# Query and key weight columns permuted at the split, so that a row's rotary partner lies in the next PSUM bank

## The chip, the cores and the metric

The kernel runs on one core of one Trainium2 chip. The metric is the device time of one execution in microseconds (us), the median of several runs.

## The reference, cut to what matters

Two layers over 4 batches of 512 tokens with 512 features, in float32. The first attends from the tokens to 1601 context rows and gates the result. The second has a causal self-attention with 16 heads of 32 features, a cross-attention and a feed-forward part. The change lies in the second layer's queries and keys:

```python
x = rms_norm(hidden_states, ln_in_w)
mixed = jnp.where(vm, x @ v_qkv, x @ l_qkv)      # two experts, chosen by token
q, k, v = jnp.split(mixed, 3, axis=-1)
...
def rotate_half(x):                               # x: ... x 32 (one head)
    d = x.shape[-1] // 2
    return jnp.concatenate([-x[..., d:], x[..., :d]], axis=-1)
...
return (q * cos + rotate_half(q) * sin, k * cos + rotate_half(k) * sin)
```

Feature f of a head (f below 16) is thus paired with feature f + 16 of the same head, and `cos` and `sin` repeat with a period of 16 features.

## The kernel before

All matrix products are made from float32 values that are split into a high and a low part (`hi`, `lo`, type fp32r), with three matmuls for each product (`three`, lines 106 to 108). The program is a sequence of stages, each a block with one instruction list for each engine; semaphores alone order the engines, and each engine takes its list in order. Between stages stands a barrier.

The stage of the change is `queries_values_keys`. It goes over the four batches in four turns (`i` = 0 to 3, batch `turns[i]`). A turn has three parts on TensorE: queries (part 0), values (part 1) and keys (part 2); the last turn takes keys before values (`place`). A part adds up eight steps (two experts of four weight tiles each) into four of the eight PSUM banks, and the parts alternate between the two halves (`bank`). In a query or key part, bank `j` ends up with features 128 j to 128 j + 127 as rows and 512 tokens as columns. For the second expert only 128 of the 512 tokens are computed here, since the branch for late tokens is taken.

The rotation of a query or key part goes as follows. ScalarE copies the four banks to `plain` (`keep_plain`, L840). TensorE multiplies each of them with the constant 128 x 128 matrix `rot`, which swaps the halves of each head and negates one, in float32, back into the same bank (`rotate`, L1097, two matmul records for each call); these calls stand between the first two steps of the next part. GpSimd forms `t1 = plain * cos_r` (`scale_pieces`, L931), with three buffers: the fourth piece has to wait until the first piece's store from `t1` has landed. VectorE multiplies the bank with `sin_r` into `plain` (L1017), adds it to `t1` (L1020), and forms the low part (L1024) after ScalarE has rounded the high part (`round_piece`, L847). SyncE stores both parts to DRAM (`store_piece`, L754 and L756), 128 rows of 2 KB at a time.

The row statistics of the norm are made meanwhile. ScalarE squares, GpSimd adds (L920), TensorE sums over the rows (`sums`, L1105) after the fourth step of the query part, ScalarE takes logarithm and exponential (`root`, L860 and L862), VectorE makes the second statistics (`second_sums`, L995 and L998) and the scaled tables (`tables`, to L1007). A little matmul (L1130) turns the row scales into a column, which VectorE copies (L1050, `rs_col`).

What lets a part begin: the query part needs the split input of its step and the value banks copied out; the value part (in the last turn the key part) needs the second statistics and all key banks of the turn before used by VectorE (`s_t2`); the key part needs all query banks used and `rs_col` copied. On ScalarE, `round_piece` of the third and fourth key piece stands behind the first `root` of the next turn.

The weights of the stage are loaded to `w_raw` (four buffers) and split: the first four tiles by VectorE at the end of the stage before (`split_tile`, L367 and L369), the other 20 by ScalarE (`round_w`, L812) and VectorE (`rest_w`, L968) in the first turn.

Of the kernel before, what the change touches and what calls it, by code (L numbers as in the profile page):

```python
# [7 lines left out]
P = 128  # L8
# [16 lines left out]
def program(nc, t, out):  # L25
# [21 lines left out]
    with ExitStack() as keep:  # L47
# [10 lines left out]
        mask_qk, mask_kq = sb("mask_qk", [P, 4, P], bf16), sb("mask_kq", [P, 4, P], bf16)  # L58
        rot = sb("rot", [P, P])
        cos_t, sin_t = sb("cos_t", [P, S]), sb("sin_t", [P, S])  # L60
# [43 lines left out]
        def three(dst, ah, al, bh, bl, start, stop, **how):  # L104

            nc.tensor.matmul(dst, ah, bh, start=start, stop=False, **how)  # L106
            nc.tensor.matmul(dst, al, bh, start=False, stop=False, **how)  # L107
            return nc.tensor.matmul(dst, ah, bl, start=False, stop=stop, **how)  # L108

        WSEMS = " ".join(f"s_wl{i}" for i in range(RAW)) + " s_wh s_ws s_wu "  # L110


        def gated_context():
# [23 lines left out]
            with ctx:  # L137
# [33 lines left out]
                with nc.Block() as block:  # L171
                    @block.sync
                    def _(sp):
# [38 lines left out]
                        for b in range(B):  # L212
                            if b:
                                sp.wait_ge(s["s_g"], 2 * DT * b)
                                sp.dma_start(fused_d[b - 1], h[:, :, :]).then_inc(s["s_up"], 16)
                            if b and b + 1 < B:
                                load_x(b + 1)
                            if b == B - 1:
                                sp.wait_ge(s["s_tl"], NB * B)
                                sp.dma_start(posi, t["pos_1xS"].broadcast_to((P, S))).then_inc(s["s_pos"], 16)  # L220
                                sp.dma_start(tpos[:, :], t["c_tpos"]).then_inc(s["s_pos"], 16)
                                sp.dma_start(tab, t["c_tab"].rearrange("(a p) c n -> p a c n", p=P)).then_inc(s["s_pos"], 16)
                                sp.dma_start(masks, t["c_masks"]).then_inc(s["s_pos"], 16)
                                sp.dma_start(tti, t["mask_BxS_ik0"][B - 1].rearrange("(a n) -> a n", a=1).broadcast_to((P, S)))\
                                    .then_inc(s["s_tt"], 16)
                                sp.dma_start(rot[:, :], t["c_rot"]).then_inc(s["s_pos"], 16)
                                sp.dma_start(sel[:, :], t["c_sel"]).then_inc(s["s_pos"], 16)
                            for p in range(2, len(PIECES)):
                                load_rows(len(PIECES) * b + p)
                            if b + 1 < B:  # L230
                                load_context(b + 1)
                                for p in range(2):
                                    load_rows(len(PIECES) * (b + 1) + p)
                        sp.wait_ge(s["s_csl"], len(PIECES) * B)
                        for n in range(DT + ET, len(tiles)):
                            load_w(sp, n, tiles[n], wl, s["s_ws"])
                        sp.wait_ge(s["s_pos"], 96)
                        sp.wait_ge(s["s_up"], 16 * (B - 1))
# [96 lines left out]
                    def _(dve):  # L335
# [21 lines left out]
                        def split_tile(n):  # L357
# [5 lines left out]
                            else:  # L363
                                hi, lo = w_hi[:, n - DT - ET, :], w_lo[:, n - DT - ET, :]
                                dve.wait_ge(s["s_gx"], DT * B)
                            dve.wait_ge(wl[n % RAW], 16 * (n // RAW + 1))
                            nc.vector.tensor_copy(hi, w_raw[:, n % RAW, :]).then_inc(s["s_wh"], 1)  # L367
                            dve.wait_ge(s["s_wh"], n + 1)
                            nc.vector.tensor_tensor(out=lo, in0=w_raw[:, n % RAW, :], in1=hi.bitcast(f32), op=ALU.subtract)\  # L369
                                .then_inc(s["s_ws"], 1)  # L370
# [21 lines left out]
                        def positions():  # L392

                            dve.wait_ge(s["s_pos"], 96)
                            nc.vector.tensor_copy(posf, posi).then_inc(s["s_hot"], 1)
# [293 lines left out]
        def queries_values_keys(more_h, more_l, k_r, q_r, v_r, s_key, s_value, s_first):  # L689

            names = ("s_tt s_k s_ku0 s_ku1 s_eu s_hin s_x s_xh s_xl s_sq s_sum s_ss s_rs s_tab s_r0u s_pl s_rot s_t1 s_t2 s_rp s_rh s_rl "
                     "s_uh0 s_uh1 s_ul0 s_ul1 s_ul2 s_rc s_rcc s_vn s_uv0 s_uv1 s_hup " + WSEMS)
# [12 lines left out]
            with ctx:  # L705
# [18 lines left out]
                def done(i, part):  # L724

                    return NT * i + G * (place(i, part) + 1)

                def split_of(n):

                    return (w_hi[:, n, :], w_lo[:, n, :]) if n < SPLIT else (more_h[:, n - SPLIT, :], more_l[:, n - SPLIT, :])  # L730

                with nc.Block() as block:
                    @block.sync
                    def _(sp):
# [14 lines left out]
                        def store_piece(o):  # L749
# [3 lines left out]
                            sp.wait_ge(s["s_rh"], o + 1)  # L753
                            sp.dma_start(dst[turns[i], 0, k * P:(k + 1) * P, :], hi[:, o % 2, :].bitcast(f32)).then_inc(s_uh[o % 2], 16)  # L754
                            sp.wait_ge(s["s_rl"], o + 1)
                            sp.dma_start(dst[turns[i], 1, k * P:(k + 1) * P, :], t1[:, o % 3, :]).then_inc(s_ul[o % 3], 16)  # L756

# [50 lines left out]
                    def _(act):  # L808
                        def round_w(n):

                            act.wait_ge(wl[n % RAW], 16 * (n // RAW))
                            nc.scalar.activation(split_of(n)[0], w_raw[:, n % RAW, :], ACT.Copy).then_inc(s["s_wh"], 1)  # L812

# [130 lines left out]
                    def _(dve):  # L944
# [64 lines left out]
                        def turn_pieces(i, group):  # L1009

                            dve.wait_ge(s["s_tab"], 5 * (i + 1))
                            for j in range(DT + 1):
                                o = 2 * DT * i + DT * group + j
                                if j < DT:
                                    dve.wait_ge(s["s_rot"], o + 1)
                                    dve.wait_ge(s["s_t1"], o + 1)
                                    nc.vector.tensor_tensor(out=plain[:, j, :], in0=ps[:, bank(3 * i + place(i, 2 * group), j), :], in1=sin_r[:, :],  # L1017
                                                            op=ALU.mult).then_inc(s["s_t2"], 1)
                                    dve.wait_ge(s["s_t2"], o + 1)
                                    nc.vector.tensor_tensor(out=t1[:, o % 3, :], in0=t1[:, o % 3, :], in1=plain[:, j, :], op=ALU.add)\  # L1020
                                        .then_inc(s["s_rp"], 1)
                                if j:
# [37 lines left out]
                    def _(pe):  # L1060
# [31 lines left out]

                        def rotate(i, group, j):

                            o = 2 * DT * i + DT * group + j
                            pe.wait_ge(s["s_pl"], o + 1)
                            nc.tensor.matmul(ps[:, bank(3 * i + place(i, 2 * group), j), :], rot[:, :], plain[:, j, :], start=True, stop=True)\  # L1097
                                .then_inc(s["s_rot"], 1)

                        def sums(i, n):  # L1100

                            pe.wait_ge(s["s_sum"], 3 * (2 * i + n + 1))
                            if i:
                                pe.wait_ge(s["s_t2"], 2 * DT * (i - 1) + DT + n + 1)
                            nc.tensor.matmul(ps[:, bank(3 * i + 1, n), :], ones[:, :], sq[:, 2 + n, :], start=True, stop=True)\  # L1105
                                .then_inc(s["s_ss"], 1)

                        def run(i, t0, steps):

                            parts = (0, 2, 1) if i == B - 1 else (0, 1, 2)  # L1110
                            for m in steps:
                                step, n = m % G, G * parts[m // G] + m % G
# [1456 lines left out]
def constants():  # L2569
# [4 lines left out]

    rot = np.zeros((P, P), np.float32)
    low = p % HD < HD // 2
    rot[p[low] + HD // 2, p[low]] = -1.0
    rot[p[~low] - HD // 2, p[~low]] = 1.0
    c["c_rot"] = rot

    c["c_sel"] = (p[:, None] == np.array([[HD * h for h in range(4)] + [HD * h + CHD for h in range(4)]])).astype(np.float32)
# [41 lines left out]
```

## Time and profile before

| | |
|---|---|
| Median of 3 runs | 2180.31 us (2179.99 to 2183.4) |
| Span of the profiled execution | 2183.6 us; no other time of that execution is listed |
| TensorE, busy share of the span | 93% |
| VectorE, ScalarE, GpSimd, busy share | 68%, 46%, 23% |
| Mean granted TensorE clock | 0.954 |
| The stage of the change | from some 358 to 620 us |

The span runs from the first to the last instruction of one profiled execution. Busy times of TensorE are modelled ends of pipelined matmuls, so distances between starts are the surer measure. A granted clock of 1.00 is the level of 2.4 GHz, one of 0.50 that of 1.2 GHz.

### The profile page before, as it was taken

To read this page: it belongs to the slowest core of one execution; us is meant where nothing else is said; L and a number is where in the kernel's file an instruction comes from. 1 tells how busy PE (TensorE), PEld (TensorE's weight loads), DVE (VectorE), ACT (ScalarE), POOL (GpSimd) and SP (SyncE) were. 2 spreads that over 40 slices of the span, in tenths; PEclk is the share of its full clock that TensorE was granted. 3 is DMA by queue.
4 is the path that set the end of the run, shared out by engine and by line. 5 is a ranking of instruction groups with operands and counts; after the bars stand their busy time and mean duration, and the time that the engine had idled before them with its cause. 6 is when DMAs were issued, how large, how long until landed. Compare 5 with 4: busy or idle time off the path is not lost. (4 is left out here: it accounts for less than half of the span.)

```text
span 2183.6 us, 32815 instructions
## 1 busy us (share of the span) xinstructions
PE 2022.3 (93%) x12701; PEld 1349.4 (62%) x12718; DVE 1492.5 (68%) x2047; ACT 1006.7 (46%) x1748; POOL 503.2 (23%) x496
## 2 busy tenths in 40 slices
PE   6999997899979997888889999999998899999997
PEld 5788874677755554677634444444434678778885
DVE  5776786566547775656579999999952565866563
ACT  1333314445415554444348888888884222221111
POOL 0321231133301212332201213222132212221211
PEclk9999998799979999999979999999999899999999
DMA  3222112333367662585544354453501433344332
GB/s 139 70 99 80 40 53 86 113 122 122 99 173 171 171 166 87 207 263 195 156 124 84 71 97 83 78 98 69 97 17 26 124 88 102 98 110 112 99 94 58
DMA packets 174936, 236.99 MB, mean 109 GB/s; under 512 B 26234, under 2 KB 103166, under 8 KB 172570
## 3 DMA queue, kind: packets, MB, share of 16 engines
q1 hardware_dynamic: 166624, 223.71, 38.2%
q0 software_dynamic: 7856, 10.90, 1.8%
q8 instruction: 113, 1.85, 0.4%
q14 instruction: 55, 0.45, 0.1%
q10 hardware_dynamic: 288, 0.08, 0.0%
HBM read 169.61 MB, written 62.91 MB: 106 GB/s over the span
## 5 line engine op out<-in xcount | busy, mean ns | idle before, releaser
L2133 ACT ACTIVATE pT_x<-ps 128x512 f32<-128x512 f32 (+1 forms) x832 | 451.3, 595 | 85.3 <-PE ps L2231 57.6
L2172 DVE TENSOR_REDUCE quarters<-ps 128x2 f32<-128x804 f32 x480 | 454.4, 992 | 46.1 <-PE ps L2203 45.0
L2246 PE MATMUL ps<-pT_x,vx_ring 128*17 128x256 f32 (+1 forms) x3328 | 261.9, 388 | 0.2 <-ACT osb_x L2115 0.2
L106 PE MATMUL ps<-mi_h,w_hi 128*128 128x512 f32 (+1 forms) x440 | 174.0, 396 | 10.5 <-DVE mi_l L2427 10.5
L2392 POOL TENSOR_TENSOR sg<-sg,keep_all 128x512 f32<-128x512 f32 (+1 forms) x55 | 87.8, 1595 | 386.5 <-ACT sg L2371 386.5
L107 PE MATMUL ps<-mi_h,w_lo 128*128 128x512 f32 (+1 forms) x440 | 173.4, 394 | 0.0
L108 PE MATMUL ps<-mi_l,w_hi 128*128 128x512 f32 (+1 forms) x440 | 172.8, 393 | 0.0
L1320 DVE TENSOR_REDUCE row_max_s<-ps 128x1 f32<-128x384 f32 (+3 forms) x176 | 109.5, 633 | 67.9 <-PE ps L1352 67.1
L1292 ACT ACTIVATE pT_s<-ps 128x512 f32<-128x512 f32 (+1 forms) x176 | 96.0, 558 | 114.9 <-PE ps L1377 112.8
L100 DVE CAST w_hi<-w_raw 128x512 fp32r<-128x512 f32 (+1 forms) x165 | 84.4, 511 | 71.5 <-PE ps L108 65.5
L2246 PEld LDWEIGHTS ps<-pT_x,vx_ring 128*17 128x17 f32 (+1 forms) x3328 | 55.6, 95 | 110.9 <-issue 68.5
L102 DVE TENSOR_TENSOR w_lo<-w_raw,w_hi 128x512 fp32r<-128x512 f32 (+1 forms) x165 | 115.8, 702 | 5.7
L2375 ACT ACTIVATE hid_h<-prod 128x512 fp32r<-128x512 f32 (+1 forms) x55 | 34.9, 634 | 177.5 <-DVE prod L2455 177.5
L2371 ACT ACTIVATE sg<-ps 128x512 f32<-128x512 f32 (+1 forms) x55 | 32.8, 596 | 164.4 <-PE ps L108 164.4
L291 ACT ACTIVATE pT<-ps 128x512 f32<-128x512 f32 (+1 forms) x52 | 31.0, 598 | 158.0 <-PE ps L108 158.0
L106 PEld LDWEIGHTS ps<-mi_h,w_hi 128*128 128x128 f32 (+1 forms) x440 | 82.3, 187 | 31.0 <-issue 11.5
L1352 PE MATMUL ps<-qkv_h,qkv_l 96*128 96x128 f32 (+3 forms) x256 | 90.5, 414 | 10.1 <-PEq L76 7.8
L108 PEld LDWEIGHTS ps<-mi_l,w_hi 128*128 128x128 f32 (+1 forms) x440 | 82.3, 187 | 20.1
L107 PEld LDWEIGHTS ps<-mi_h,w_lo 128*128 128x128 f32 (+1 forms) x440 | 82.3, 187 | 18.8
L2455 DVE TENSOR_TENSOR prod<-ps,sg 128x512 f32<-128x512 f32 (+1 forms) x55 | 37.9, 690 | 78.8 <-PE ps L108 70.0
L106 PE MATMUL ps<-hid_h,w_hi 128*128 128x512 f32 (+1 forms) x220 | 87.9, 400 | 3.0 <-DVE hid_l L2459 3.0
L331 POOL TENSOR_TENSOR sin_t<-sin_t,pT 128x512 f32<-128x512 f32 (+1 forms) x48 | 72.4, 1509 | 65.0 <-ACT pT L291 64.4
(350 smaller groups left out, 4816.6 us busy)
## 6 DMA issues: line engine op xcount, KB each, us to landing
qkv_l<-self_q_by_part SPq DMA_DIRECT2D x48, 256.0 KB, 4.5
qkv_h<-self_k_by_part SPq DMA_DIRECT2D x48, 256.0 KB, 6.6
w_raw<-L_xattn_l_gate SPq DMA_DIRECT2D x40, 256.0 KB, 2.9
w_raw<-L_xattn_l_up SPq DMA_DIRECT2D x40, 256.0 KB, 2.9
w_raw<-L_xattn_l_down SPq DMA_DIRECT2D x40, 256.0 KB, 2.7
kx_first<-cross_k_by_part SPq DMA_DIRECT2D x36, 200.2 KB, 6.7
cross_v_by_group<-v_aug SPq DMA_DIRECT2D x16, 442.0 KB, 3.8
vx_ring<-cross_v_by_group SPq DMA_DIRECT2D x16, 442.0 KB, 10.0
```

What stands on the lines that cost most here:

```text
L100: nc.vector.tensor_copy(hi, raw).then_inc(s_high, 1)
L102: nc.vector.tensor_tensor(out=lo, in0=raw, in1=hi.bitcast(f32), op=ALU.subtract).then_inc(s_split, 1)
L106: nc.tensor.matmul(dst, ah, bh, start=start, stop=False, **how)
L107: nc.tensor.matmul(dst, al, bh, start=False, stop=False, **how)
L108: return nc.tensor.matmul(dst, ah, bl, start=False, stop=stop, **how)
L1292: nc.scalar.activation(pT[:, u % 3, j:j + n, 0:width], heads_of(ps[:, SCORES + v % 3, :], n, width), ACT.Exp, scale=SCALE).then_inc(s["s_e ...
L1320: nc.vector.tensor_reduce(out=row_max[:, g % 2, j:j + heads, q], in_=heads_of(bank, heads, (q + 1) * P), axis=AX.X, op=ALU.max)\
L1352: last = nc.tensor.matmul(bank[:, m * width:(m + 1) * width], q_r[0:STACK, at + m, cut], k_r[0:STACK, at + m, 0:width], start=False, stop= ...
L2133: nc.scalar.activation(pT[0:kn, u % 3, j, :], ps[0:kn, 5 + v % 3, :], ACT.Exp, scale=SCALE)\
L2172: nc.vector.tensor_reduce(out=quarters[:, g % 2, pair, :, q, quarter], in_=ps[:, at:at + 2, 0:MAXW], axis=AX.X, op=ALU.max)\
L2246: last = nc.tensor.matmul(ps[j * HD:j * HD + CHD + 1, 4, queries], v_r[0:kn, g % RING, kt, j, :], pT[0:kn, u % 3, j, queries], start=kt == ...
L2392: nc.gpsimd.tensor_tensor(out=by_batch(sg[0:cn, c % 2, :]), in0=by_batch(sg[0:cn, c % 2, :]), in1=keep_all[0:cn, experts[i], :, rows(i)], ...
```

## The change

The columns of the query and key weights are written in another order when they are split: column 64 a + 16 q + r goes to column 128 q + 16 a + r (`p (a q r) -> p q a r`, with a below 8, q below 4, r below 16). Bank q then holds the features 64 a + 16 q + r, in row 16 a + r. The partner of a row lies in the same row of bank `q ^ 1`, and the tables need no change, as they depend on r alone. VectorE reads the partner's bank directly (L1017) and adds or subtracts (L1020). The rotation matmuls, the matrix `rot` and its load are gone. The stores put the rows back in their old places in DRAM, so that everything behind the stage is as it was. Two waits of TensorE now ask for the second used bank, and VectorE waits for the copy of the neighbouring bank ahead of an even piece.

```diff
+        def by_piece(w):
+            return w.rearrange("p (a q r) -> p q a r", q=DT, r=HD // 2)
...
-                                sp.dma_start(rot[:, :], t["c_rot"]).then_inc(s["s_pos"], 16)
...
+                            raw = w_raw[:, n % RAW, :]
+                            if n >= DT + ET:
+                                raw, hi, lo = by_piece(raw), *(w.rearrange("p (q a r) -> p q a r", q=DT, r=HD // 2) for w in (hi, lo))
-                            nc.vector.tensor_copy(hi, w_raw[:, n % RAW, :]).then_inc(s["s_wh"], 1)
+                            nc.vector.tensor_copy(hi, raw).then_inc(s["s_wh"], 1)
...
+                def piece_rows(dst, i, part, j):
+                    return dst[turns[i], part].rearrange("(a q r) n -> q a r n", q=DT, r=HD // 2)[j]
+                def raw_of(n):
+                    raw = w_raw[:, n % RAW, :]
+                    return raw if n // G == 1 else by_piece(raw)
+                def as_raw(w, n):
+                    return w if n // G == 1 else w.rearrange("p (q a r) -> p q a r", q=DT, r=HD // 2)
...
-                            sp.dma_start(dst[turns[i], 0, k * P:(k + 1) * P, :], hi[:, o % 2, :].bitcast(f32)).then_inc(s_uh[o % 2], 16)
+                            sp.dma_start(piece_rows(dst, i, 0, k), hi[:, o % 2, :].bitcast(f32)).then_inc(s_uh[o % 2], 16)
-                            sp.dma_start(dst[turns[i], 1, k * P:(k + 1) * P, :], t1[:, o % 3, :]).then_inc(s_ul[o % 3], 16)
+                            sp.dma_start(piece_rows(dst, i, 1, k), t1[:, o % 3, :]).then_inc(s_ul[o % 3], 16)
...
-                            nc.scalar.activation(split_of(n)[0], w_raw[:, n % RAW, :], ACT.Copy).then_inc(s["s_wh"], 1)
+                            nc.scalar.activation(as_raw(split_of(n)[0], n), raw_of(n), ACT.Copy).then_inc(s["s_wh"], 1)
...
-                            nc.vector.tensor_tensor(out=lo_, in0=w_raw[:, n % RAW, :], in1=hi_.bitcast(f32), op=ALU.subtract)\
+                            nc.vector.tensor_tensor(out=as_raw(lo_, n), in0=raw_of(n), in1=as_raw(hi_.bitcast(f32), n), op=ALU.subtract)\
...
-                                    dve.wait_ge(s["s_rot"], o + 1)
                                     dve.wait_ge(s["s_t1"], o + 1)
-                                    nc.vector.tensor_tensor(out=plain[:, j, :], in0=ps[:, bank(3 * i + place(i, 2 * group), j), :], in1=sin_r[:, :],
-                                                            op=ALU.mult).then_inc(s["s_t2"], 1)
+                                    if j % 2 == 0:
+                                        dve.wait_ge(s["s_pl"], o + 2)
+                                    nc.vector.tensor_tensor(out=plain[:, j, :], in0=ps[:, bank(3 * i + place(i, 2 * group), j ^ 1), :],
+                                                            in1=sin_r[:, :], op=ALU.mult).then_inc(s["s_t2"], 1)
...
+                                                            op=ALU.add if j % 2 else ALU.subtract).then_inc(s["s_rp"], 1)
...
-                                pe.wait_ge(s["s_t2"], 2 * DT * (i - 1) + DT + n + 1)
+                                pe.wait_ge(s["s_t2"], 2 * DT * (i - 1) + DT + 2)
...
-                                if m < 2 and i:
-                                    rotate(i - 1, 1, 2 * m)
-                                    rotate(i - 1, 1, 2 * m + 1)
...
-                                if m // G == 1 and step < 2:
-                                    rotate(i, 0, 2 * step)
-                                    rotate(i, 0, 2 * step + 1)
-                                if i == B - 1 and m // G == 2 and step < 2:
-                                    rotate(i, 1, 2 * step)
-                                    rotate(i, 1, 2 * step + 1)
...
-                                    pe.wait_ge(s["s_t2"], 2 * DT * i + DT * (place(i, 1) - 1) + 1)
+                                    pe.wait_ge(s["s_t2"], 2 * DT * i + DT * (place(i, 1) - 1) + 2)
```

## Rows read from the trace of the kernel before

**Rows 1.** The page, the span in 40 slices, TensorE's busy tenths.
```profile
PE   6999997899979997888889999999998899999997
```

**Rows 2.** Windows: stretch, length, busy time of each engine, clock, DMA share, GB/s.
```profile
530.00:560.00 30.00, 29.45 (x154) 24.14 (x153) 21.73 (x29) 15.21 (x26) 10.85 (x8) 1.00 0.28 97
```

**Rows 3.** Grouped lines of 330 to 625 us: busy us, mean ns, idle before.
```profile
L1097 PE MATMUL ps<-plain,rot 128*128 128x512 f32 x64 | 30.7, 602 | 2.2 <-ACT plain L840 2.2
...
L968 DVE TENSOR_TENSOR qkv_l<-w_raw,qkv_h 128x512 fp32r<-128x512 f32 x20 | 19.7, 1016 | 16.6 <-ACT qkv_h L812 16.6
```

**Rows 4.** Timeline of TensorE around two pairs of rotations: start, length, instruction.
```profile
442.75 1.98 PE L1097 MATMUL ps<-plain,rot 128*128 128x512 f32 x4 [0.55 <-ACT plain L840]
...
447.12 0.40 PE L108 MATMUL ps<-xe0l,w_hi 128*128 128x512 f32 x1
447.36 1.88 PE L1097 MATMUL ps<-plain,rot 128*128 128x512 f32 x4
...
449.30 0.40 PE L107 MATMUL ps<-xe0h,w_lo 128*128 128x512 f32 x1
```

**Rows 5.** Timeline of TensorE, third and fourth turn: first matmuls of parts, sums.
```profile
496.74 0.45 PE L106 MATMUL ps<-xe0h,w_hi 128*128 128x512 f32 x1
...
512.23 1.88 PE L1105 MATMUL ps<-sq,ones 128*128 128x512 f32 x4
...
519.26 0.46 PE L106 MATMUL ps<-qkv_h,xe0h 128*128 128x512 f32 x1
...
538.09 0.39 PE L106 MATMUL ps<-xe0h,qkv_h 128*128 128x512 f32 x1
...
554.28 0.45 PE L106 MATMUL ps<-xe0h,w_hi 128*128 128x512 f32 x1
...
576.80 0.46 PE L106 MATMUL ps<-xe0h,qkv_h 128*128 128x512 f32 x1
...
597.03 0.45 PE L106 MATMUL ps<-qkv_h,xe0h 128*128 128x512 f32 x1
```

**Rows 6.** Timelines of ScalarE, GpSimd and VectorE, third turn, query part.
```profile
513.29 0.69 ACT L860 ACTIVATE rs<-ps,eps_col 128x512 f32<-128x512 f32 x1 [4.73 <-PE ps L1105]
...
515.83 1.14 ACT L847 ACTIVATE rows_h<-t 128x512 fp32r<-128x512 f32 x2
...
509.45 1.29 POOL L931 TENSOR_TENSOR t<-plain,cos_r 128x512 f32<-128x512 f32 x1 [3.40 <-DMA self_k_by_part<-t]
...
511.57 0.69 DVE L1020 TENSOR_TENSOR t<-t,plain 128x512 f32<-128x512 f32 x1
516.47 1.29 DVE L1024 TENSOR_TENSOR t<-t,rows_h 128x512 fp32r<-128x512 f32 x2 [4.21 <-ACT rows_h L847]
...
518.47 0.69 DVE L998 TENSOR_TENSOR rs<-rs,ps 128x512 f32<-128x512 f32 x1
```

**Rows 7.** Timeline of VectorE, third turn, end of the value part.
```profile
534.33 1.47 DVE L1024 TENSOR_TENSOR t<-t,rows_h 128x512 fp32r<-128x512 f32 x2
536.03 0.16 DVE L1050 COPY rs_col<-ps 128x4 f32<-128x4 f32 x1 [0.24 <-PE ps L1130]
```

**Rows 8.** DMA issues (size, median us to landing), and a window within one store.
```profile
qkv_l<-self_q_by_part SPq DMA_DIRECT2D x48, 256.0 KB, 4.5
...
self_k_by_part<-t SPq DMA_DIRECT2D x16, 256.0 KB, 2.1
...
564.20:564.40 0.20, 0.20 (x2) 0.17 (x1) 0.20 (x1) 0.20 (x1) 0.00 (x0) 1.00 0.99 379
```

**Rows 9.** Two gaps of TensorE in the timeline, and windows behind them.
```profile
342.00 0.51 PE L106 MATMUL ps<-cn_h,w_h 128*128 128x512 f32 x1 [2.17 <-DVE cn_l L510]
...
345.00:352.00 7.00, 7.00 (x32) 5.63 (x31) 2.56 (x4) 2.75 (x4) 0.00 (x0) 1.00 0.00 0
...
421.30 0.47 PE L106 MATMUL ps<-xe0h,qkv_h 128*128 128x512 f32 x1 [1.83 <-DVE rs_col L1050]
...
422.50:426.00 3.50, 3.50 (x10) 2.71 (x9) 2.20 (x5) 0.01 (x1) 0.00 (x0) 0.52 0.75 230
```

More of the change, by code:

```diff
@@ L58, in program @@
         mask_qk, mask_kq = sb("mask_qk", [P, 4, P], bf16), sb("mask_kq", [P, 4, P], bf16)
-        rot = sb("rot", [P, P])
         cos_t, sin_t = sb("cos_t", [P, S]), sb("sin_t", [P, S])
@@ L236, in _ @@
                             load_w(sp, n, tiles[n], wl, s["s_ws"])
-                        sp.wait_ge(s["s_pos"], 96)
+                        sp.wait_ge(s["s_pos"], 80)
                         sp.wait_ge(s["s_up"], 16 * (B - 1))
@@ L366, in split_tile @@
                             dve.wait_ge(wl[n % RAW], 16 * (n // RAW + 1))
-                            nc.vector.tensor_copy(hi, w_raw[:, n % RAW, :]).then_inc(s["s_wh"], 1)
+                            raw = w_raw[:, n % RAW, :]
+                            if n >= DT + ET:
+                                raw, hi, lo = by_piece(raw), *(w.rearrange("p (q a r) -> p q a r", q=DT, r=HD // 2) for w in (hi, lo))
+                            nc.vector.tensor_copy(hi, raw).then_inc(s["s_wh"], 1)
                             dve.wait_ge(s["s_wh"], n + 1)
-                            nc.vector.tensor_tensor(out=lo, in0=w_raw[:, n % RAW, :], in1=hi.bitcast(f32), op=ALU.subtract)\
+                            nc.vector.tensor_tensor(out=lo, in0=raw, in1=hi.bitcast(f32), op=ALU.subtract)\
                                 .then_inc(s["s_ws"], 1)
@@ L392, in positions @@
                         def positions():
-                            dve.wait_ge(s["s_pos"], 96)
+                            dve.wait_ge(s["s_pos"], 80)
                             nc.vector.tensor_copy(posf, posi).then_inc(s["s_hot"], 1)
@@ L689, in queries_values_keys @@
         def queries_values_keys(more_h, more_l, k_r, q_r, v_r, s_key, s_value, s_first):
-            names = ("s_tt s_k s_ku0 s_ku1 s_eu s_hin s_x s_xh s_xl s_sq s_sum s_ss s_rs s_tab s_r0u s_pl s_rot s_t1 s_t2 s_rp s_rh s_rl "
+            names = ("s_tt s_k s_ku0 s_ku1 s_eu s_hin s_x s_xh s_xl s_sq s_sum s_ss s_rs s_tab s_r0u s_pl s_t1 s_t2 s_rp s_rh s_rl "
                      "s_uh0 s_uh1 s_ul0 s_ul1 s_ul2 s_rc s_rcc s_vn s_uv0 s_uv1 s_hup " + WSEMS)
@@ L1014, in turn_pieces @@
                                 if j < DT:
-                                    dve.wait_ge(s["s_rot"], o + 1)
                                     dve.wait_ge(s["s_t1"], o + 1)
-                                    nc.vector.tensor_tensor(out=plain[:, j, :], in0=ps[:, bank(3 * i + place(i, 2 * group), j), :], in1=sin_r[:, :],
-                                                            op=ALU.mult).then_inc(s["s_t2"], 1)
+                                    if j % 2 == 0:
+                                        dve.wait_ge(s["s_pl"], o + 2)
+                                    nc.vector.tensor_tensor(out=plain[:, j, :], in0=ps[:, bank(3 * i + place(i, 2 * group), j ^ 1), :],
+                                                            in1=sin_r[:, :], op=ALU.mult).then_inc(s["s_t2"], 1)
                                     dve.wait_ge(s["s_t2"], o + 1)
-                                    nc.vector.tensor_tensor(out=t1[:, o % 3, :], in0=t1[:, o % 3, :], in1=plain[:, j, :], op=ALU.add)\
-                                        .then_inc(s["s_rp"], 1)
+                                    nc.vector.tensor_tensor(out=t1[:, o % 3, :], in0=t1[:, o % 3, :], in1=plain[:, j, :],
+                                                            op=ALU.add if j % 2 else ALU.subtract).then_inc(s["s_rp"], 1)
                                 if j:
@@ L1091, in project @@
                             last.then_inc(s["s_wu"], 1)
[L1093 to L1098, printed above, removed]
                         def sums(i, n):
@@ L1111, in run @@
                             for m in steps:
-                                step, n = m % G, G * parts[m // G] + m % G
+                                n = G * parts[m // G] + m % G
                                 project(i, n, t0)
-                                if m < 2 and i:
-                                    rotate(i - 1, 1, 2 * m)
-                                    rotate(i - 1, 1, 2 * m + 1)
                                 if m == 3:
@@ L2573, in constants @@
     c = {"c_ident": np.eye(P, dtype=np.float32)}
[L2575 to L2579, printed above, removed]
     c["c_sel"] = (p[:, None] == np.array([[HD * h for h in range(4)] + [HD * h + CHD for h in range(4)]])).astype(np.float32)
```

## The prediction

> **What bounds the kernel now.** I read the page's slices first [rows 1]: TensorE is at 9 tenths in most of the 40 slices, the other engines nowhere for long, so the question is whether it is also the bound in the one stage that the diff touches. That stage (queries, values, keys of the self-attention) runs from about 358 to 620 us, in four turns of three parts each. In a stretch of its steady turns TensorE works 29.45 of 30.00 us at full clock, VectorE 21.73, ScalarE 15.21, GpSimd 10.85 [rows 2]. The grouped lines then give the size of what goes: 64 matmul records (two for each of 32 rotations), 30.7 us busy, and 2.2 us of waiting ahead of them [rows 3]. The timeline of TensorE shows that they stand in its stream like any other matmul, and where each part begins [rows 4, 5]; the timelines of the other engines show when the next part could begin [rows 6, 7]. The reader is to see that the parts start when TensorE is ready, but that the hand-back of PSUM banks follows closely.
>
> **What the removed work costs.** A pair of rotations lies between a matmul that starts at 447.12 and one at 449.30, with one projection matmul behind the pair: 2.18 us, less two normal steps of 0.23 each, is 1.71 us [rows 4]. There are 16 pairs: 27.4 us. With the waits of 2.2 us ahead of seven of them [rows 3], 29.6 us is the most that can come back. It comes back only where the next part can start earlier, so I walk through a steady turn, the third (its query part starts at 496.74 [rows 5]).
>
> **Query part to value part.** The value part waits for the row statistics (the second L998 result), which VectorE ends at 518.47 + 0.69 = 519.16; it starts at 519.26 [rows 5, 6]. VectorE reaches that result late because of a queue on ScalarE: the rounding of pieces 3 and 4 stands behind the logarithm, which waited 4.73 us for the sums of TensorE, and these stand behind both pairs of rotations [rows 5, 6]. Without them the sums move from 512.23 to 508.26 (2 x 1.71 and the wait of 0.55 [rows 4]); logarithm, rounding and statistics follow, 3.97 us earlier, to 515.2. What is late next is the last piece itself: its addition ends at 511.57 + 0.69 = 512.26 whatever TensorE does, because GpSimd waited 3.40 us for the store that frees its buffer [rows 6]; rounding (0.6) and the 2.19 us from its end (515.83 + 1.14) to the statistics give 515.1. TensorE itself would be ready at 519.26 - 3.97 = 515.29. So all 3.97 us come back, with about 0.1 us to spare.
>
> **Value part to key part.** The key part needs VectorE to have used all query banks and to have copied the row scales. VectorE ends its pieces at 534.33 + 1.47 = 535.80 [rows 7], 16.64 us behind the statistics, in a chain through ScalarE, GpSimd and a store in which no rotation is waited for; with the copy (0.16) and a semaphore it is 16.9. The key part could then start at 515.2 + 16.9 = 532.1 instead of 538.09: 6.0 us for the turn. TensorE is ready at 515.29 + 18.83 - 3.6 = 530.5, so 1.6 us of the second two pairs turn into a wait for VectorE. The key part holds no rotation and keeps its 16.19 us (538.09 to 554.28 [rows 5]).
>
> **The moved store.** A piece's 128 rows now go to eight blocks of 16 rows in DRAM, where they went to one block. A store of the old form fills its engines (share 0.99) and moves 256 KB in some 0.68 us at 379 GB/s, landing 2.1 us after its issue [rows 8]. No row shows the new form. Below it costs nothing (same bytes, same 2 KB rows); above, the nearest row is the load that gathers the same 256 KB in pieces from the same tensor: 4.5 us [rows 8], 2.4 more. I take 0.7 us, a doubled transfer, nearer to the store's own row because the loads come in bursts of six that queue behind each other. This lies on the path twice in a turn: the fourth product of GpSimd waits for the first store. The statistics come 0.6 us later (the spare 0.1 taken off), the row scales 0.7 more: 6.0 becomes 4.7 us in turns two and three. The row shows 16 engines at work. The Trainium skill, DMA: Bandwidth & Descriptors, section "Why a DMA increments its semaphore by 16 and not by 1", says that a transfer is spread over the largest count up to 16 that divides the outermost size of both sides; eight blocks would then use 8 engines. By that rule the sum is the one below; by the old store's row unchanged, it is 3.9 us better (0.7 + 1.3 + 1.3 + 0.6 over the turns); no run here shows it yet.
>
> **First and last turn.** The first key part already waits 1.83 us for the row scales [rows 9]. Its chain is set by VectorE's weight splits and a store, so the two pairs removed ahead of it only widen the gap to 5.3 us: gain 0, less 0.7 for the store. The last turn has keys before values: its query part gives 3.4; its key part (two pairs and a short wait, 3.6) has the banks in time, as VectorE has used them before 534.33, 15.2 us behind the statistics [rows 6, 7], and the part runs 597.03 - 576.80 - 3.6 = 16.6 [rows 5]; its value part gives 3.4. Together 10.4 us. What follows the stage (stores, barrier, loads) shifts as it is.
>
> **The clock.** After the gap of 1.83 us the granted clock was 0.52 (the 1.2 GHz level) for 3.5 us; after one of 2.17 us it stayed at 1.00 [rows 9]. At 0.52 the stretch loses 0.48 x 3.5 = 1.7 us. The new gaps are some 2.2 us in turns two and three and 5.3 us in the first. I charge 1.7 for one of the two, as one of the two rows fell, and 1.7 for the longer one: 3.4 us. Below 0, above 5.1.
>
> **The rest, at nothing.** The splits of the 16 permuted tiles handle as many elements as before, in runs of 16. No row shows that form; below it is free, above I double the mean of 1016 ns [rows 3]: eight tiles lie ahead of the first turn's pieces, at most 8.1 us. I take 0, since the element count sets the even duration of these rows. The added VectorE wait (the neighbour's eviction before an even piece) is covered by GpSimd's product of 1.29 us [rows 6], longer than one ScalarE pass (0.69 at most [rows 6]); uncovered, the subtraction, the remainder and the store behind it would wait too. The sums now wait for two used banks; the second is used long before 508. The dropped load of the rotation matrix (64 KB, one SP issue) lies among loads with slack.
>
> **The sum.** -0.7 + 4.7 + 4.7 + 10.4 - 3.4 = 15.7 us. The profiled execution spans 2183.6 us, 3.3 above the median of the runs (2180.31) and level with the slowest, 2183.4; its span becomes 2167.9, and the median 2164.6.
>
> **The rivals.**
> - *The store lands as before and the gaps leave the clock alone*: 0 + 6.0 + 6.0 + 11.0 = 23.0, 2157.3 us. For it: bytes and row length are unchanged, and one gap of 2.17 did no harm. Against: the other did. Chance 0.2.
> - *The store lands as late as the piecewise loads* (+2.4 us): the turns give -2.4, 1.3, 1.3, 8.7, less 3.4 for the clock: 5.5, 2174.8. Much the same would come of doubled splits (15.7 - 8.1 = 7.6, 2172.7). Together 0.18.
> - *The rotations were not on the path*: if the parts were paced by VectorE, SP's queue or the stores throughout, removal makes idle time only, and the time is 2180. Against: TensorE shows no idle ahead of the value part or the key part of the steady turns [rows 5]. Chance 0.04.
> - *Slower: the clock does not come back.* The rotations closed gaps; without them each key part of the first three turns begins after a wait. If its clock then stays at the 1.2 GHz level through the whole part, 16.19 us of work take about 15 us more, 45 in all: 2180.3 - 19.1 + 45 = 2206. It decides from 19.1 / 3 = 6.4 us lost in each, that is some 13 us at that level, four times the stretch of [rows 9]. Chance 0.06.
>
> My forecast has 0.5, and its own range is 2160 to 2169; 0.02 is left for what I don't see. The range that leaves out no more than 2 in 10 reaches from the best case to the doubled splits: 2156 to 2173. A measurement of this kernel tells about 0.2% (4.4 us) from no change. Faster by more: the first two cases and nearly all of the third, 0.89; within: 0.04; slower: 0.07.
>
> **What would show it.** Right: no rotation records; each steady turn (key start to key start) some 53 us instead of 57.5; the sums directly behind the fourth step; a wait of 1.5 to 2.5 us for the row-scale copy ahead of the key part in turns two and three, over 4 us in the first; none in the last turn. The store step is judged by the landing of the first store of a part (2.1 or 2.8 us) and by the DMA share while it runs (1.0 or 0.5); the split step by the mean of L968's successor. Wrong: low clock through key parts, a wait ahead of value parts over 1 us, splits above 1.3 us each, or an unchanged turn.

## The result and the profile after the change

The changed kernel takes 2202.39 us (median of 4 runs, 2199.21 to 2204.67) against 2180.88 for the one before (4 runs): a ratio of 1.0094, 95% interval 1.0079 to 1.0108. It is 1% slower; 2164.6 us had been forecast, with 2156 to 2173 as the range. The profiled execution took 2204.67 us (span 2202.7).

The rotations are gone, and nothing stands in their place on TensorE. Yet the third turn, query start to query start, is 62.24 us long where [rows 5] give 57.54. The timeline of the changed kernel for that turn, TensorE first, then ScalarE, GpSimd, VectorE and SyncE's issues (start, length, instruction, idle time before it and what ended that):

```profile
500.12 0.45 PE L105 MATMUL ps<-xe0h,w_hi 128*128 128x512 f32 x1
513.46 2.73 PE L1117 MATMUL ps<-sq,ones 128*128 128x512 f32 x4 [1.91 <-DVE plain L1036]
518.01 0.47 PE L105 MATMUL ps<-xe1h,qkv_h 128*128 128x128 f32 x1 [1.82 <-issue]
528.30 0.73 PE L105 MATMUL ps<-qkv_h,xe0h 128*128 128x512 f32 x1
546.07 0.47 PE L105 MATMUL ps<-xe0h,qkv_h 128*128 128x512 f32 x1 [1.20 <-DVE rs_col L1069]
562.36 0.46 PE L105 MATMUL ps<-xe0h,w_hi 128*128 128x512 f32 x1
...
640.87 1.31 PE L1355 MATMUL ps<-qkv_h,qkv_l 96*128 96x128 f32 x4 [18.25 <-PEq L75]
...
492.02 1.41 ACT L890 ACTIVATE v_nat<-ps,rs_col 128x512 f32<-128x512 f32 x2 [6.98 <-DMA self_v_by_group<-v_nat]
...
509.65 4.19 POOL L949 TENSOR_TENSOR t<-plain,cos_r 128x512 f32<-128x512 f32 x3
520.59 1.27 POOL L949 TENSOR_TENSOR t<-plain,cos_r 128x512 f32<-128x512 f32 x1 [6.75 <-DMA self_k_by_part<-t]
...
525.40 0.69 DVE L1016 TENSOR_TENSOR rs<-rs,ps 128x512 f32<-128x512 f32 x1
...
513.40 0.59 SPq L772 DMA_DIRECT2D self_k_by_part<-rows_h  x1
```

From the timelines of before, the lines to hold against it (ScalarE just ahead of the third turn, GpSimd in it, TensorE at the end of the stage):

```profile
483.97 1.42 ACT L872 ACTIVATE v_nat<-ps,rs_col 128x512 f32<-128x512 f32 x2 [1.96 <-DMA self_v_by_group<-v_nat]
...
501.81 4.24 POOL L931 TENSOR_TENSOR t<-plain,cos_r 128x512 f32<-128x512 f32 x3
...
623.39 1.31 PE L1352 MATMUL ps<-qkv_h,qkv_l 96*128 96x128 f32 x4 [7.76 <-PEq L76]
```

Read the first timeline from the bottom up. A store costs SyncE 0.59 us to issue. GpSimd's fourth product waits 6.75 us for the first store, where it waited 3.40 [rows 6]; the statistics end at 526.09, 25.97 us into the turn (22.42 before [rows 5, 6]). The value stores stand behind these stores on SyncE's list, so ScalarE waits 6.98 us for a value buffer (1.96 before). Behind that wait stand the next turn's rounding and squares: GpSimd's first product starts 9.53 us into the turn (5.07 before). So VectorE frees the banks late, and the statistics' matmuls wait 1.91 us for them. Behind them a second gap opens, 1.82 us that the view calls issue. The windows of the same kernel show what follows these gaps (stretch, length, busy time of each engine, granted clock, DMA share, GB/s):

```profile
515.20:515.40 0.20, 0.20 (x2) 0.00 (x0) 0.20 (x1) 0.20 (x1) 0.00 (x0) 0.50 0.60 102
518.01:528.30 10.29, 10.29 (x48) 10.29 (x49) 3.96 (x6) 5.55 (x8) 1.27 (x1) 0.50 0.49 142
```

The second expert of the query part runs its whole 10.29 us at a granted clock of 0.50, the 1.2 GHz level; that part took 5.71 us before (519.26 less the 513.55 at which it began, 1.32 us behind the sums of [rows 5]). While stores run, the DMA share is 0.5 to 0.6, at 102 GB/s in a stretch within a store, where [rows 8] show 0.99 and 379. At the end of the stage TensorE waits 18.25 us for the next stage's first matmul, where it waited 7.76.

### The profile page after: what moved, and what is told of

Read it like the earlier page. It is cut to its first block and busy times, and to the rows that moved or that the text cites. A ratio compares the mean times of both kernels' runs of the same rounds, so it can differ in the third digit from the quotient of the medians.

```text
span 2202.7 us, 32670 instructions
## 1 busy us (share of the span) xinstructions
PE 2015.3 (91%) x12637; PEld 1355.2 (62%) x12654; DVE 1489.8 (68%) x2047; ACT 1007.1 (46%) x1748; POOL 505.2 (23%) x496
```

## The experiments

My theory: the stores into eight blocks cost all of it. First rival: the rotations' absence does (gaps, a lower clock, the read from the neighbouring bank). Second rival: the permuted splits do.

The runs below came in four groups, and the kernel before was timed in each of them: its medians are 2180.4, 2182.3, 2184.4 and 2183.4 us. A ratio is taken within a group; a difference of two medians from different groups is sure to some 4 us only.

**The old stores, the rest of the change kept.** The output rows of the stage stay in permuted order.

```diff
-return dst[turns[i], part].rearrange("(a q r) n -> q a r n", q=DT, r=HD // 2)[j]
+return dst[turns[i], part, j * P:(j + 1) * P, :]
```

> The changed kernel, but each 128-row piece of queries and keys goes to its old contiguous place in HBM, so the rows of the next stage stand in the permuted order. Theory 'stores' (the eight-block stores are what costs): the multiply on GpSimd waits again about as before, the loss goes and the gain of the rotations stays, 2155 to 2170 us. Rival 'rotations' (the gaps and the lower clock that their absence leaves on TensorE, or the read of the other bank): 2190 us or more. Rival 'splits' (strided split of the weights): 2195 us or more.

Measured: 2165.69 us, ratio 0.9927 (0.9911 to 0.9944). The timeline of TensorE in its third turn and at the start of the next stage, with the fourth product of GpSimd, and windows of the second expert in turns two, three and four:

```profile
494.46 0.45 PE L105 MATMUL ps<-xe0h,w_hi 128*128 128x512 f32 x1
...
507.99 0.32 PE L105 MATMUL ps<-xe1h,qkv_h 128*128 128x128 f32 x1 [0.39 <-issue]
...
513.52 0.50 PE L105 MATMUL ps<-qkv_h,xe0h 128*128 128x512 f32 x1
...
530.26 0.47 PE L105 MATMUL ps<-xe0h,qkv_h 128*128 128x512 f32 x1 [1.65 <-DVE rs_col L1069]
...
546.56 0.45 PE L105 MATMUL ps<-xe0h,w_hi 128*128 128x512 f32 x1
...
609.20 1.09 PE L1355 MATMUL ps<-qkv_h,qkv_l 96*128 96x128 f32 x3 [10.45 <-PEq L75]
...
507.96 1.27 POOL L949 TENSOR_TENSOR t<-plain,cos_r 128x512 f32<-128x512 f32 x1 [4.05 <-DMA self_k_by_part<-t]
```

```profile
453.12:461.20 8.08, 8.07 (x49) 8.08 (x49) 3.96 (x6) 4.89 (x7) 1.28 (x1) 0.65 0.69 231
507.99:513.52 5.53, 5.53 (x48) 5.42 (x48) 3.96 (x6) 3.86 (x6) 1.25 (x1) 1.00 0.49 185
561.76:567.38 5.62, 5.57 (x49) 5.44 (x49) 3.96 (x6) 3.27 (x6) 1.29 (x1) 1.00 0.52 191
```

The turn is 52.10 us, and the second expert of the third turn takes 5.53 us at full clock. The change without its stores gains 15 us: both rivals fall as the cause of the loss. ScalarE's and VectorE's splits have means of 626 and 1017 ns, as before. The second turn gained much less, 56.26 us (438.20 to 494.46) against 57.57 before: the first window shows its second expert at a mean clock of 0.65.

**The stores alone.** The kernel before, rotations kept, with the eight-block addresses (the next stage then finds the rows in another order).

```diff
-sp.dma_start(dst[turns[i], 0, k * P:(k + 1) * P, :], ...)
+sp.dma_start(piece_rows(dst, i, 0, k), ...)
```

> The kernel before, rotations and all, with only the addresses of the query and key stores changed to the eight blocks of 16 rows. Theory 'stores': the same landing times of 6 to 7 us as in the changed kernel and most of its loss against the forecast, 2195 to 2220 us. Rivals 'rotations' and 'splits': 2179 to 2186 us, the store being hidden where the rotations are still there.

Measured: 2208.95 us, ratio 1.0137 (1.0117 to 1.0158), 28.6 us over the 2180.4 of before. The stores cost this much with rotations and 2202.39 - 2165.69 = 36.7 us without: the rotations covered some 8 us of it.

**What makes such a store slow.** A block in front of the stage stores tiles with nothing else running, two one at a time and two together in each layout.

```diff
+for (n, k, rows, pitch), d in zip(layouts, probes):
+    for m in range(2):
+        sp.dma_start(to(m), h[:, m, :]).then_inc(s_probe, 16)
+        done += 16
+        sp.wait_ge(s_probe, done)
```

> The kernel before with a small block ahead of the query/key/value stage, in which SyncE stores one 128x512 tile at a time and waits for it, then two at once, in six layouts: 128 contiguous rows; 8 blocks of 16 rows at 64, 66 and 32 rows pitch; 16 blocks of 8 rows at 64 rows pitch; 16 frequencies of 8 rows 64 rows apart. If only the engine count matters: single landings about 2.1 us contiguous and about 2.8 us for all three eight-block layouts (0.7 us of transfer doubled), both sixteen-block layouts as the contiguous one. If the power-of-two pitch matters: 66 rows lands clearly earlier than 64 and 32 rows. The time itself only grows by the probe.

Measured: 2251.63 us, a single run with the block's own time in it; only its trace is read here. The issues of the two single stores of each layout (duration min, median, max; first and last start; the three layouts of eight blocks share a row), then windows in a single store of a contiguous piece, twice in one of eight blocks, and in a pair of eight-block stores:

```profile
L2540 SPq DMA_DIRECT2D probe_eight<-h x6: 565/565/722, 362.9 to 394.4; - x6
L2540 SPq DMA_DIRECT2D probe_line<-h x2: 327/327/327, 356.1 to 358.2; - x2
L2540 SPq DMA_DIRECT2D probe_sixteen<-h x2: 552/564/577, 404.0 to 406.9; - x2
L2540 SPq DMA_DIRECT2D probe_rowmajor<-h x2: 518/518/518, 413.8 to 416.7; - x2
```

```profile
361.20:361.40 0.20, 0.00 (x0) 0.00 (x0) 0.00 (x0) 0.00 (x0) 0.00 (x0) 0.50 1.07 399
364.40:365.40 1.00, 0.00 (x0) 0.00 (x0) 0.00 (x0) 0.00 (x0) 0.00 (x0) 0.50 0.49 47
366.20:366.60 0.40, 0.00 (x0) 0.00 (x0) 0.00 (x0) 0.00 (x0) 0.00 (x0) 0.50 0.43 164
...
374.50:375.50 1.00, 0.00 (x0) 0.00 (x0) 0.00 (x0) 0.00 (x0) 0.00 (x0) 0.50 0.52 184
```

As each single store waits for the one before, the distance of two starts is a store's whole time: 2.0 us contiguous, 2.9 in both layouts of sixteen (expected as contiguous). In the timeline of SyncE the eight-block pairs are 4.25, 4.06 and 4.05 us apart for pitches of 64, 66 and 32 rows, where 2.8 us had been expected: the power-of-two pitch is not it. An eight-block store never goes much over half the DMA share, and at first it moves only 47 GB/s at that share. So the halving was right, as far as it went, but a slow start of over 1 us and a longer issue come on top. What makes the start slow stays open. In the halving the trace agrees with the rule that the prediction took from the Trainium skill, DMA: Bandwidth & Descriptors, "Why a DMA increments its semaphore by 16 and not by 1".

**Sixteen in place of eight.** Frequency major, head minor within a bank; tables repeated instead of tiled.

```diff
-w.rearrange("p (a q r) -> p q a r", ...)   # store "(a q r) n -> q a r n"
+w.rearrange("p (a q r) -> p q r a", ...)   # store "(a q r) n -> q r a n"
...
```

> The changed kernel with another order inside a bank: rotary frequency major, heads minor, so that a store walks 16 frequencies of 8 rows each (outermost count 16 in place of 8, same 64-row pitch of the inner step), and the split reads weight columns 64 apart. If the count of the outermost blocks is what slows the store (half of the DMA engines): landing as before, 2156 to 2170 us. If the pitch of 128 KB is what slows it: landing of 5 us or more and 2195 us or more. If the absence of the rotations costs: 2190 us or more. If the strided column read of the split costs: the split rows on ScalarE and VectorE lengthen, and the first turn alone is longer.

Measured: 2181.78 us, ratio 1.0006 (0.9993 to 1.0020). The stores land in 2.9 to 3.1 us (2.1 to 2.4 before), and 20.6 of the 36.7 us come back, fewer than expected for the count alone. TensorE still waits 13.03 us at the end of the stage, and the splits now pay: from its first query to its first key matmul the first turn takes 65.50 us, against 61.44 with the old stores. The grouped lines of the splits (busy us, mean ns):

```profile
L986 DVE TENSOR_TENSOR qkv_l<-w_raw,qkv_h 128x512 fp32r<-128x512 f32 x20 | 24.3, 1260 | 14.2 <-ACT qkv_h L830 14.2
L830 ACT ACTIVATE qkv_h<-w_raw 128x512 fp32r<-128x512 f32 x20 | 18.2, 937 | 1.9 <-DMA w_raw<-L_xattn_v_qkv 1.9
```

**Where the slow stores bite.** A fourth buffer for the turned rows, eight-block stores kept:

```diff
-t1 = sb("t1", [P, 3, S], ...)
+t1 = sb("t1", [P, 4, S], ...)
...
```

> The changed kernel, eight-block stores and all, with a fourth buffer for the turned rows (t1), so that GpSimd's fourth product of a group no longer waits for the group's first store. If that wait is how the stores cost time inside the turns: GpSimd's waits for stores of 6 to 8 us go, about 5 us of each of the three later turns come back, and the late end of the stage stays, 2180 to 2190 us. If the wait only moves to ScalarE's rounding, which waits for its own store, or to the value stores queued behind on SyncE's list: 2195 to 2204 us.

Measured: 2185.9 us, ratio 1.0015 (1.0001 to 1.0029): 16.5 us come back. GpSimd's waits for these stores fall from 38.5 and 28.4 us in all to 3.3 and none, while ScalarE's rounding now waits 15.8 and 17.4 us for its own store and the late end stays (15.90 us). The buffer does more than undo the slow stores: before the change these waits were 22.0 and 15.1 us, and with contiguous stores the same buffer is worth 9.6 us (2165.52 to 2155.95, below). So of the 16.5 us perhaps only 16.5 - 9.6 = 6.9 are the slow stores' (an estimate, as that pair of runs differs in other things too).

**The end of the stage.** Old stores in the last turn alone (those rows stand in permuted order):

```diff
+if i == B - 1:
+    return dst[turns[i], part, j * P:(j + 1) * P, :]
```

> The changed kernel with eight-block stores in the first three turns and the old contiguous stores in the last turn (whose rows the next stage then finds in the permuted order). In the trace TensorE waits 18.25 us for the next stage's first matmul, against 7.76 us before the change and 10.45 us with all the old stores. If the late end of the stage is a cost of its own, beside the waits in the turns: 7 to 12 us come back, 2190 to 2196 us. If the wait on the buffer in the earlier turns is all: 2198 to 2204 us.

Measured: 2190.63 us, ratio 1.0041 (1.0027 to 1.0056): 11.8 us come back. TensorE's wait at the border is as before the change (7.76 us):

```profile
628.62 0.59 PE L1354 MATMUL ps<-mask_qk,ident_b 128*128 128x512 bf16 x1 [7.77 <-PEq L75]
```

**The gap called issue.** The old stores, and the early-flag branch taken out of TensorE's list: the path that this input takes is always taken.

```diff
-early = nc.tensor.value_load(early_v[...])
-with nc.tensor.If(early > 0):
-    run(i, 0, range(DT, 3 * G))
-with nc.tensor.If(early < 1):
-    run(i, S - P, range(DT, 3 * G))
+run(i, S - P, range(DT, 3 * G))
```

> The run with the old stores (rows in the permuted order), and TensorE's list in turns 2 to 4 without the load of the early flag and the two branches: the path that this input takes is always taken. If the idle 0.4 to 2.1 us between the statistics' matmuls and the second expert, which the rotations used to cover, is the branch, they go, with some of the stretches at the lower clock behind them: 2156 to 2163 us. If it is hidden by the later wait for VectorE's row scales: 2164 to 2168 us, as with the branch.

Measured: 2158.21 us, ratio 0.9891 (0.9873 to 0.9909), 7.5 us under the run with the branch. In its second turn the second expert follows the sums at once:

```profile
443.75 1.88 PE L1117 MATMUL ps<-sq,ones 128*128 128x512 f32 x4
445.07 0.62 PE L105 MATMUL ps<-xe1h,qkv_h 128*128 128x128 f32 x1
```

So the gaps of 0.39 to 2.07 us in the run with the old stores are the branch, and the clock adds to them: behind the gap of 1.79 us ahead of 453.12, the second expert of the second turn lost 2.5 us at a mean clock of 0.65. But not all of the 7.5 us was brought about by the change. The kernel before has the gap too, in its first turn, where no rotations stand ahead of the statistics:

```profile
389.53 0.44 PE L106 MATMUL ps<-xe1h,qkv_h 128*128 128x128 f32 x1 [6.37 <-issue]
```

Without the branch this gap is gone as well. From the first matmul of the stage to that of the next the trace without the branch is 11.97 us shorter than that with it (the two profiled executions lie further apart than the medians), and 5.34 of these lie in the first turn.

**Contiguous stores with the rows in an order that the loads can use.** Within a pair of banks the rotary index is major and the head minor; the loads of the next stage take runs of 4 heads.

```diff
-w.rearrange("p (a q r) -> p q a r", q=DT, r=HD // 2)
+w.rearrange("p (q a d) -> p q d a", q=2, d=HD)
-src[b, part, rows, :].rearrange("(j d) n -> d j n", d=HD)
+src[b, part].rearrange("(q d a) n -> q d a n", q=2, d=HD)[q, :, a:a + 4, :]
```

> A correct version whose stores are the old contiguous ones: weight columns of a head pair of banks in the order (rotary index major, head minor), partner still in the next bank, and the next stage's loads take 4 heads as 8 KB runs at 16 KB pitch. Theory 'stores' with the row-major run's splits (0.94 and 1.26 us in place of 0.63 and 1.02 us for columns read at a stride): as the run with the old stores, plus 4 to 8 us in the first turn, 2168 to 2176 us. If this shorter stride costs the splits nothing: 2161 to 2168 us. If the changed loads are what the next stage feels: its first matmuls wait for keys and queries and it is 2180 us or more.

Measured: 2177.44 us, ratio 0.9977 (0.9964 to 0.9990). The splits take 942 and 1252 ns here, and the way to the first key matmul takes 65.50 us again, 4.1 more than with the old stores. The stage also starts later in this trace (364.96 us against 357.82), but two kernels below with the same splits start it at 359.22 and 361.50, so the splits alone do not set it. What makes up the rest of the 11.8 us lost against the old stores was not tried by itself.

**First halves in banks 0 and 1, second halves in 2 and 3.**

```diff
+"p (h f r) -> p f h r"   # partner bank j ^ 2; 12 loads of 128 KB per group
```

> Another correct version with contiguous stores: first halves of all heads in banks 0 and 1, second halves in banks 2 and 3, so the partner lies two banks on; runs of 16 columns in the splits, as in the changed kernel; the next stage's loads of queries and keys are 12 of 128 KB per group in place of 6 of 256 KB. If the splits stay at 0.63 and 1.02 us and the loads have slack: 2163 to 2172 us. If VectorE's start, one or two ScalarE copies later per group, or the doubled loads at the stage's border show: 2172 to 2180 us.

Measured: 2226.38 us, ratio 1.0205 (1.0185 to 1.0224): my bounds did not hold. With the partner two banks on, the second of the statistics' matmuls waits 2.5 us for VectorE, the branch follows, and the second expert is at the low clock again; the stage's end comes 22.8 us later than with the old stores (632.04 against 609.20). The other 38 us lie behind the stage, where the loads are twice as many; that these are the cause was not tried alone.

**The branch ahead of the sums.** On the head-minor version, the statistics' matmuls move behind the branch, into both arms.

```diff
-project(i, n, t0)
-if m == 3:
-    sums(i, 0); sums(i, 1)
+if m == DT:
+    sums(i, 0); sums(i, 1)
+project(i, n, t0)
```

> The correct version with contiguous stores and head-minor columns, with one order changed: on TensorE's list the statistics' matmuls of a turn stand behind the early-flag branch, inside both of its arms, in place of ahead of it, so that TensorE's sequencer can take the branch while the first expert's matmuls still run. Theory 'the exposed branch' (7.5 us by the run without it): the idle time between the statistics and the second expert goes, 2168 to 2172 us. If the sequencer cannot get that far ahead, or the statistics start later for it: 2175 to 2181 us.

Measured: 2165.52 us, ratio 0.9918 (0.9903 to 0.9933), 11.9 us under the same version with the old order: more than expected. The gap in the first turn goes too.

**With the fourth buffer as well.**

```diff
-t1 = sb("t1", [P, 3, S], ...)
+t1 = sb("t1", [P, 4, S], ...)
...
```

> The run with the branch ahead of the statistics, and a fourth buffer for the turned rows. With stores of 2.1 to 2.3 us, GpSimd's waits for a store (some 40 us in all, 1.5 to 4 us at a time) go; if VectorE's chain behind them sets the row scales, which the keys wait for in some turns, 2 to 6 us of the kernel go: 2163 to 2169 us. If TensorE's own work is the bound by then: the same as without the buffer within 2 us.

Measured: 2155.95 us, ratio 0.9878 (0.9861 to 0.9896), the fastest of all, and faster than I expected. From key start to key start a turn takes 51.55 us, no wait in it is over 1.04 us, and the second expert stays at full clock; timeline and window:

```profile
472.32 0.47 PE L105 MATMUL ps<-xe0h,qkv_h 128*128 128x512 f32 x1 [1.04 <-DVE rs_col L1072]
...
501.55 0.62 PE L105 MATMUL ps<-xe1h,qkv_h 128*128 128x128 f32 x1
...
507.73 0.50 PE L105 MATMUL ps<-qkv_h,xe0h 128*128 128x512 f32 x1 [0.30 <-DVE rs L1019]
...
523.87 0.47 PE L105 MATMUL ps<-xe0h,qkv_h 128*128 128x512 f32 x1 [1.02 <-DVE rs_col L1072]
```

```profile
501.55:507.40 5.85, 5.85 (x50) 5.49 (x48) 5.45 (x9) 5.16 (x7) 0.00 (x0) 1.00 0.62 234
```

**Both mends on the eight-block stores.** The changed kernel with these two edits:

```diff
-if m == 3:          # behind project(i, n, t0)
+if m == DT:         # ahead of project(i, n, t0)
     sums(i, 0); sums(i, 1)
-t1 = sb("t1", [P, 3, S], ...)
+t1 = sb("t1", [P, 4, S], ...)
...
```

> The changed kernel with its eight-block stores, with both mends: a fourth buffer for the turned rows and the branch ahead of the statistics. If the two costs add (16.5 us for the wait on the buffer, 7.5 us for the branch): 2176 to 2181 us. If the slow stores still hold up ScalarE's rounding and the value stores so that the gap is only moved: 2183 to 2188 us, as with the buffer alone.

Measured: 2176.58 us, ratio 0.9964 (0.9951 to 0.9978): against 2202.39 that is 25.8 us, as expected if the two costs add (16.5 and, behind it, 9.3). The contiguous stores with their order of rows are worth another 20.6 us.

The kernel before was not run with these two edits. Its first turn has the branch gap and its GpSimd waits for stores as well, so they may help it too, and how much of the way from 2180.4 to 2155.95 us is the permutation's own stays open.

## Why the prediction was wrong, step by step

- **What the removed work costs, and the walk through the turn**: right in the third turn. With the old stores the query part of the third turn takes 513.52 - 494.46 = 19.06 us (forecast 22.52 - 3.97 = 18.55, the 0.39 gap not foreseen), the value part 16.74 (forecast 532.1 - 515.2 = 16.9), the key part 16.30 (16.19), and a wait of 1.65 us for the row scales stands where 1.6 was forecast. In the second turn 1.3 us came back in place of 6.0, for the branch and the clock below.
- **The moved store**: this step failed, in its size and in its places. I took 0.7 us, a doubled transfer, and bounded it at 2.4. A lone eight-block store takes 2.0 to 2.2 us more; on the path GpSimd's wait grew by 3.35 us. And I let the delay act at one place in a part, GpSimd's fourth product. In the runs a buffer more at that place is worth 16.5 of the 36.7 us (6.9 of them by the low estimate above), and old stores in the last turn, which mend the end of the stage, 11.8; the rest fits ScalarE's waits for its own buffer and for the value stores behind on SyncE's list, which no run changed alone. The two prices may overlap, as the buffer also shortened the end a little.
- **First and last turn**, "what follows the stage shifts as it is": wrong. The wait at the border grew from 7.76 to 18.25 us, and to 10.45 even with the old stores, since the last stores, not TensorE, release the next stage. With the old stores the border moved 623.39 - 609.20 = 14.2 us, 0.7 of which lie ahead of the stage.
- **The clock**: I charged 3.4 us, for gaps ahead of the key part. With the old stores the first key part (its first expert 13.63 us against 10.99 in the third turn), the second turn's query part (8.08 against 5.53) and its value part (13.16 against 11.02) lose 7.3, of which the first key part lost 1.6 before the change too (it took 12.56). With the slow stores three second experts (9.83, 10.29 and 10.29 against 5.53) alone lose 13.8. The rival "the clock does not come back" had this mechanism and the right sign, but placed it in the key parts; it sits in the query part, behind the statistics, and the stores and the branch bring it about. That its 2206 us came near the 2202.39 measured is chance.
- **Missing altogether**: the branch behind the statistics. Before the change no gap stands there in turns two to four; without the rotations it does. That the rotations let TensorE's sequencer get to the branch early fits this, and that the gaps go when the branch stands ahead of the statistics, but no row here shows when the sequencer reaches it. Branch and clock together cost 7.5 us, and by the traces a little over half of that (11.97 - 5.34 = 6.6 of 11.97) came with the change. My sum gives 2160.7 for an unchanged store (2157.3 and the 3.4 us of the clock); with the old stores it was 2165.7. The 2158.2 without the branch does not bear the sum out, as it also leaves out the first turn's gap, which the sum kept.
- **The splits at nothing, the bank read and VectorE's added wait**: right for runs of 16 columns, with the means unchanged (VectorE's read of the neighbouring bank takes 686 ns with the old stores, 685 before). The reason given for the splits, that the element count sets their duration, does not hold: the same elements took VectorE 1260 ns when read 64 columns apart.

## What to carry to other kernels

Price a moved store at every place where something waits for it or queues behind it (buffer ring, issuing queue, end of stage), and look at its outermost count before calling its bytes unchanged: here a cheaper matmul stream was paid back twice over by the DMA pattern that it asked for. When work goes from an in-order engine, ask what its sequencer did meanwhile, since a branch or a semaphore wait that it hid comes into the open and can bring the clock down behind it. Where a layout must change, let the side with slack pay: order the rows so that the waited-for store stays contiguous and the loads take the new pattern, in as many transfers as before: the version with twice as many loads was the slowest of those compared here, though the loads were not tried alone.

## What the runs showed of the hardware that I had not expected

- A 256 KB store to eight blocks of 16 rows takes 4.05 to 4.25 us alone, one of 128 contiguous rows 2.0, sixteen blocks 2.9, with no clear difference between pitches of 64, 66 and 32 rows; its issue takes SyncE 0.565 in place of 0.327 us.
- ScalarE's and VectorE's splits of fp32 columns cost nothing extra in runs of 16 (626 and 1017 ns), but 937 and 1260 ns when they read columns 64 apart, and 942 and 1252 at 32 apart.
- After gaps of 1.91 and 1.82 us close together TensorE ran 10.29 us at the low level without a pause, while after one of 0.39 us it ran at full clock. The length of a gap alone does not tell: with the old stores the clock was 0.65 on the mean behind a gap of 1.79 us (453.12) and 1.00 behind one of 2.07 us (561.76).
